# Drawing the first half of the next batch's linear attention into the last feed-forward of the batch before, with all four batches on one time axis

## The reference

```python
x = layernorm(x + linear_attention(x))       # 8 heads of 16: silu(q), silu(k), rotation, decay mask
x = layernorm(x + local_transformer(x))      # 2 layers: window attention (8 heads of 64, window 64) + gated FFN
x = layernorm(x + deformable_attention(x))   # 33 samples per token, positions computed from x, linear interpolation
x = layernorm(x + moe(x))                    # 8 experts, softmax over the sequence, top 2

# deformable attention, per batch:
pos = clip(t + (s - 16) * freq_avg[t] + phase_avg[t], 0, L - 1)      # s = 0..32
lo = floor(pos); frac = pos - lo
g = x[lo] + frac * (x[lo + 1] - x[lo])                               # a gather of rows of x
out = silu(sum_s(g * w[t, s, head]) @ out_w.T)
```

## Time and profile before

| | us |
|---|---|
| median of 3 runs | 2317.84 (2312.19 to 2323.54) |
| the profiled execution, its own time | 2323.0 |
| its span, first to last instruction | 2321.0 |
| PE / DVE / ACT / POOL busy | 1669.0 / 1307.1 / 969.2 / 1140.6 |
| of POOL's, the 1056 gathers (L744) | 1074.9 |
| mean granted TensorE clock | 0.853 |

### The profile page before, as it was taken

The page is one execution under the profiler, slowest core; times in us unless marked ns, Lnnn a source line. Parts: engine busy times, 40 slices in busy tenths (PEclk is TensorE's granted clock), DMA queues, the critical chain, the costliest instruction groups (busy, mean ns, idle before and its releaser), DMA issues.

```text
span 2321.0 us, 34040 instructions
## 1 busy us (share of the span) xinstructions
PE 1669.0 (72%) x11753; PEld 1075.6 (46%) x11753; DVE 1307.1 (56%) x2182; ACT 969.2 (42%) x2341; POOL 1140.6 (49%) x1136
## 2 busy tenths in 40 slices
PE   5667675766687767756878758667777567999967
PEld 3343333434454534435545424355445335766747
DVE  6664643567766734667577436576666344343333
ACT  3355553323445553225444623145455333343431
POOL 0000003467766516477676062776763265777710
PEclk8899997878898978779899978788998778999975
DMA  3000003223333323133333231333333252333311
GB/s 126 10 19 14 14 15 64 64 82 110 114 90 90 94 42 89 50 101 112 98 103 101 42 76 43 101 110 101 101 94 73 46 152 67 103 102 102 102 23 37
DMA packets 92404, 178.45 MB, mean 77 GB/s; under 512 B 21434, under 2 KB 49220, under 8 KB 91972
## 3 DMA queue, kind: packets, MB, share of 16 engines
q0 software_dynamic: 50688, 138.48, 21.4%
q1 hardware_dynamic: 41540, 37.70, 5.8%
HBM read 150.93 MB, written 8.92 MB: 69 GB/s over the span
## 4 chain that ended last, share of the span: by engine, by line
PE 33%; DVE 22%; POOL 15%; issue 14%; ACT 11%; DMA 4%; DVEq 0%; POOLq 0%; SPq 0%; ACTq 0%
POOL pool_c L744 14%; PE c L1591 4%; DVE pool_c L1240 4%; DMA pool_c<-rows_of_x,idx 4%; ACT prob L881 3%; DVE ssq L1144 3%; DVE nmax L1154 2%; PE pb L1491 2%; PE pa L1491 2%; DVE pool_a L1197 2%; PE tb L1372 2%; PE pb L1539 2%; PE pa L1539 2%; PE sc L1656 2%; PE pa L1529 1%
## 5 line engine op out<-in xcount | busy, mean ns | idle before, releaser
L744 POOL DMA_INDIRECT pool_c<-rows_of_x,idx x1056 | 1074.9, 1018 | 1070.7 <-issue 655.9
L1240 DVE TENSOR_TENSOR pool_c<-pool_c 128x768 f32<-128x768 f32 x352 | 341.0, 974 | 307.3 <-DMA pool_c<-rows_of_x,idx 268.5
L1591 PE MATMUL c<-ident,pool_c 128*128 128x128 f32 x2112 | 338.1, 305 | 171.3 <-DVE pool_c L1240 171.1
L1591 PEld LDWEIGHTS c<-ident,pool_c 128*128 128x128 f32 x2112 | 278.8, 158 | 298.9 <-DVE pool_c L1240 211.2
L881 ACT ACTIVATE prob<-sc,nmax 128x128 f32<-128x128 f32 x512 | 180.3, 379 | 126.9 <-DVE nmax L1154 126.8
L796 ACT COPY pool_a<-tb 128x512 f32<-128x512 f32 x188 | 112.1, 596 | 69.6 <-PE tb L1372 69.6
L1491 PE MATMUL pa<-wqkv,pool_a 128*128 128x512 f32 x192 | 115.7, 688 | 16.1 <-DVE pool_a L1197 6.9
L1491 PE MATMUL pb<-wqkv,pool_a 128*128 128x512 f32 x192 | 116.4, 693 | 13.3 <-DVE pool_a L1010 6.4
L1521 PE MATMUL ta<-vmix,pool_a 128*64 128x64 f32 x1024 | 79.0, 236 | 62.0 <-ACT pool_a L796 60.1
L881 ACT ACTIVATION_READ_ACCUMULATOR prob<-sc,nmax 128x1 f32 x512 | 111.4, 218 | 0.0
L1144 DVE TENSOR_REDUCE ssq<-pool_a 128x16 f32<-128x1024 f32 x64 | 77.7, 1214 | 57.8 <-ACT pool_a L857 57.7
(11 more groups left out here) (404 smaller groups left out, 3354.9 us busy)
## 6 DMA issues: line engine op xcount, KB each, us to landing
pool_c<-rows_of_x,idx POOLq DMA_INDIRECT x1056
vmix<-vring SPq DMA_DIRECT2D x128, 128.0 KB
rows_of_x<-x2tok SPq DMA_DIRECT2D x16, 256.0 KB
xtok<-in_x SPq DMA_DIRECT2D x4, 512.0 KB, 4.4
x_of_all<-x2tok SPq DMA_DIRECT2D x8, 256.0 KB, 2.4
out<-pool_c SPq DMA_DIRECT2D x8, 256.0 KB, 2.6
wqkv<-in_wqkv SPq DMA_DIRECT2D x1, 1536.0 KB
xtok<-x_of_all SPq DMA_DIRECT2D x3, 512.0 KB, 6.3
```

The source lines that it names most:

```text
L744: pool.indirect_dma_start(gat[:, n % GB, s, :], None, table, bass.IndirectOffsetOnAxis(ap=idx[:, t, SC * c + s:SC * c + s + 1], axis=0),). ...
L1240: V.tensor_tensor(g4, g4, wv, ALU.mult).then_inc(SEM["c_prod"], 1)
L1591: ins = mm(out[:, c:c + P], x, ident[:], start=(i == 0 and k == 0), stop=(i == BCH - 1 and k == len(parts) - 1), is_transpose=True, skip_g ...
```

## The change

All batches are put on one axis, with batch b at 29.0 x b, and the whole program is written out: the loop, its register arithmetic and its branches are gone, and every wait compares with a constant. On this axis the opening's early half stands at 20.0 to 23.0 of the batch before and its late half at 23.0 to 27.0 (that is -6.0 to -2.0 of its own batch). The head of block 1 moves to 20.8 to 22.8 and chunks 9 to 87 to 22.8 to 44.0 (-6.2 to 15.0 of the next batch). A few offsets within a tile change. x turned over gets a tensor of its own (`xin`) in place of `xb`; `pool_a` is laid out anew, so that `silu4`, `keyA`, `qryA` and `vp` lie where window attention's buffers come free first, with waits for those. The norms of the opening get semaphores of their own. Four small tensors of the mixture of experts move into `pool_a`.

```diff
-OPENING = 7.66
+PERIOD = 29.0
+OPENING, LATE_OPENING, TAIL_AT = 7.0, 4.0, 22.0
...
-    "pe": {... "O": 1.49, "turn": -0.5, ...},
-    "act": {... "rn": -1.84, "P": 1.17, ... "turn": -0.35, ...},
-    "dve": {... "rn": -1.99, ... "O": 1.45, ...},
+    "pe": {... "O": 1.46, "turn": -0.45, ...},
+    "act": {... "P": 1.17, "rn": -1.72, ... "turn": -0.3, ...},
+    "dve": {... "rn": -1.87, ... "O": 1.3, ...},
...
-HEAD_AT, GATHER_AT, GATHER_END = -6.87, -4.81, 15.0
+HEAD_AT, GATHER_AT, GATHER_END = 20.8, 22.8, 44.0
 NEXT_AT, NEXT_GATHER, NEXT_END = 17.3, 18.98, 20.78
...
+    k = opening.index(("KV",))
     for i, step in enumerate(opening):
-        out.append((-2.0 - OPENING * (1 - i / len(opening)) + at["opening"], step))
+        if i < k:
+            time = -2.0 - OPENING + (OPENING - LATE_OPENING) * i / k
+        else:
+            time = -2.0 - LATE_OPENING * (1 - (i - k) / (len(opening) - k))
+        out.append((time + at["opening"], step))
...
+    for b in range(B):
+        out += [(PERIOD * b + time, ("first", b, *step)) for time, step in first_times(e)]
+        out += [(PERIOD * b + time, ("second", b, *step)) for time, step in second_times() if b < B - 1 or time < TAIL_AT]
+    return [step for _, step in sorted(out, key=lambda x: x[0])] + tail_steps()
...
-            for s in FIRST[order]:
-                first_or_ahead(0, *s)
-            with eng.Fori(1, B) as b:
-                for part_, *s in both_steps(order):
...
+            for part_, b, *s in schedule(order):
+                if part_ == "first":
+                    first(b, *s)
...
+        silu4 = part("a", 4, BLK)
+        ktok = silu4.rearrange("p a (b c) -> p (a b) c", b=2)
         keyA = part("a", G, N)
         qryA = part("a", G, N)
-        silu4 = part("a", 4, BLK)
-        ktok = silu4.rearrange("p a (b c) -> p (a b) c", b=2)
+        vp = part("a", T, H, 2 * HD)
...
-        hT = part("b", N)
         sq = part("b", 2, BLK)
         qn = part("b", 2, HB, DH)
         r2 = part("b", 2, HB, DH)
+        hT = part("b", N)
...
-                    wait_filled(pool, ("up", LAYERS - 1, J - 1, FB - 1), b - 1)
+                    wait_filled(pool, ("O", LAYERS - 1, T - 1), b - 1)
                     nc.gpsimd.memset(vp[:], 0.0).then_inc(SEM["a_zero"], 1)
...
-                        copy_out(("xT", j), xb[:, 1 + BLK * j:1 + BLK * (j + 1)], b)
+                        if j == 0:
+                            wait_drained(act, ("ao", J - 1), b - 1)
+                        copy_out(("xT", j), xin[:, BLK * j:BLK * (j + 1)], b)
...
+                    wait(act, "b_qk", b - 1, LAYERS * T)
                     wait(act, "a_rot", b, i - 3)
...
+                    if i == 0:
+                        wait_filled(dve, ("vp", LAYERS - 1, T - 1), b - 1)
+                    elif i == 4:
+                        wait_filled(dve, ("S", LAYERS - 1, T - 1), b - 1)
                     wait_drained(dve, ("kq", i), b)
...
                 elif what == "KV":
+                    wait_filled(dve, ("up", LAYERS - 1, J - 1, FB - 1), b - 1)
```

More of the change, by code:

```diff
@@ L512, in build @@
         }
-        AHEAD = {n for n in PER if n[:2] == "c_" and not n.startswith("c_gather")}
         SEM = {n: ctx.enter_context(nc.semaphore(n)) for n in PER}
@@ L1134, in first @@
                     if l == 0:
[L1135 removed]
+                        wait_norm(dve, "out", j, b)
                     else:
```

289 lines of the change are left out of this document (128 added, 161 removed), and 6 rows, old and new, of the table AT.

## The result

The changed kernel takes 2288.19 us (median of 4 runs, 2275.92 to 2293.16), the kernel before beside it 2319.44 (2312.19 to 2323.54). The ratio is 0.9855, its 95% interval 0.9818 to 0.9891. The gain is 31 us, where 75 were predicted. The profiled execution took 2293.16 us with a span of 2291.3.

What follows compares the result with a forecast made beforehand. POOL was taken to pace `KV` to the sixth maximum except for one 37.5 us hole. Per seam -24 - 1 = -25 us, three seams -75, from 2323.0 to 2248, less 5.2 for the median: 2243 us; range 2198 to 2303.

Steps and rivals of the forecast that it cites:

- inner one: Range of the likeliest case alone, 2208 to 2285 us; that case had 58%.
- main term: Late opening: `acc` 9 moves right behind `E` 0; `KV` to sixth maximum 173 us against 197.3, 24 less per seam.
- the branches: Loop branches at the seams, removed by writing out: 1 us less per seam on average.
- hole: POOL's one gap of 37.5 us behind `KV`, waiting for PE, which reaches `acc` 9 only behind `heads` 3.
- small waits in the measured proportion: POOL's waits from `KV` to sixth maximum, scaled from 5.1 us per 38.3 chunks: 5.3 us.
- no gap over 10 us: Sign of being right: POOL has no such gap between the first row numbers and the sixth maximum.
- Early half and head: Row numbers to `KV`: four early steps save at most 5 us, block 1's head costs 6; zero, -6 to +10.
- Offsets and the last stretch: `rn` behind the copies of `P`, and the stretch after the sixth maximum: zero each.
- The rival of the slower side: `rn`'s new place lengthens every tile by up to 1.5 us, 96 us over 64 tiles: 2339 us; 9%.
- Batch 0 and tail: They hold nothing of the seam but one head: zero, -3 to +3 us.
- The opening's own chain: Rival: PE, ACT and DVE bind the opening, `KV` to projection 70 us; 2294 us with the head's full cost; 17%.
- Gathers slower beside DVE: Rival: mean gather in the denser opening rises to 1.25 us, costing 25 us more, main term gone: 2315 us; 8%.

Runs made afterwards that it cites:

- small products: The changed kernel with DVE's product of each chunk cut to its first sixth (128 values of 768 a partition): 2206.71 us, one execution.

## Why the prediction was partly right

The forecast was 75 us less, the measurement is 31 us less. The 2288 us lie inside the range of 2198 to 2303 and above the inner one of 2208 to 2285. That inner range doesn't come out of its own terms: 20 to 33 us for the main term, 1 for the branches and +2 as the middle of -6 and +10 give 2222 to 2261. Over the three seams of the profiled executions `KV` to the sixth maximum gave 36.5 us where 72 were forecast, and row numbers to `KV` took 9.6 more where 3 less were forecast. The rest of the passes gave 9.8 where zero was forecast, and batch 0 and the tail took 7.1 more. That the last two nearly cancel is luck. I had taken batch 2 for all three; batch 1's hole was 33.4 us, and it gave only 9.2.

**Direction and the bound: right.** POOL paces `KV` to the sixth maximum, except for its holes. Its rate of 4.08 us a chunk came out at 4.09, a third fewer gathers shortened the stretch by 30 us, and where the holes are closed its own work fills 175.2 of 179.2 us.

**The main term: mechanism right, size wrong.** Forecast were 173 us, made of 162.8 own work, 5.3 small waits and 5 to the restart. The trace has 183.9: 166.3, 10.8 and 6.8 (917.80 to 924.58). So -24 became -13. Of the 10.9 missing, 7.3 are waits. The step that failed is "small waits in the measured proportion". I had looked only at where `acc` 9 goes. `acc` 10 is tied to `E` 1, and so to DVE's scan: the gap of 7.02 us at 935.04. A buffer comes free where the chain of the opening lets it. The other 3.5 are 0.8 chunks more than my 39.9. The hole is not worth its length either: with both chunks put ahead, POOL waits 8.0 us less than with the head alone behind, and the stretch is 5.0 shorter in batch 2 and 2.9 in the mean, as POOL does more chunks in it. So waits and chunks aren't two separate terms, as my sum has them. My sign "no gap over 10 us" was met at 9.50 and told nothing; the length of the stretch was the test.

**Early half and head: zero forecast, +2.3 measured (+4.5 and +2.8 in batches 1 and 3).** The parts were near: I set the head at 6 us and the run has 7.3, the four early steps at 5 saved, and the kernel with the head behind is 5.2 under the 63.0 of before. The error is in what the term was held against. The head's way back into the late half costs nothing in the faster groups, so with it the order of the seam is worth 33 to 38 us, and the change gave some 20 of them away. I wrote that its removal there isn't counted, and did not ask whether it should have moved at all. The tables came to three loads more in the whole (109 for 106), and taking one away gave 0.5 us: inside the bounds. The kernel with the head behind `KV` even has 115 of them and is 16 us shorter. The Trainium skill (ScalarE: Activation LUTs, What ACT_TABLE_LOAD costs) has 2.66 us for a switch. Here all 109 loads take 1.28 us; 66 of the next instructions start within 0.03 us of the load's end, and the others wait for PE or DVE.

**Branches: right, a little small.** -3 forecast, -7 measured for the whole form (-11 to -3), in which the branches aren't told from the new layout.

**Offsets and the last stretch: zero forecast, wrong twice.** `rn` behind `P` gives about 14 us in the whole and costs 4 to 7 in batch 0. The rival of the slower side had the right place and the wrong mechanism and, for the whole, the wrong sign. `rn` isn't held up tile by tile: in 15 of batch 0's 16 tiles it starts within 0.13 us of DVE's sum. The other, at 0.8, is one in which a feed-forward has changed the table. ACT in order of time there, the changed kernel:

```profile
250.61 0.60 ACT L763 COPY pool_a<-tb 128x512 f32<-128x512 f32 x1
251.23 1.28 ACT L834 ACT_TABLE_LOAD   x1
252.53 0.22 ACT L834 ACTIVATE ssq<-ssq 128x16 f32<-128x16 f32 x1
252.76 1.28 ACT L836 ACT_TABLE_LOAD   x1
254.06 0.31 ACT L836 ACTIVATE ssq<-ssq,cols 128x16 f32<-128x16 f32 x1
```

and the kernel before:

```profile
249.50 1.28 ACT L863 ACT_TABLE_LOAD   x1
250.98 0.21 ACT L863 ACTIVATE ssq<-ssq 128x16 f32<-128x16 f32 x1 [0.20 <-DVE ssq L1146]
251.21 1.28 ACT L865 ACT_TABLE_LOAD   x1
```

Before, the first load passes while ACT waits for DVE's sum (0.20 us are left of the wait). Now the two copies stand in that wait, and the load comes behind it. That explains 0.8 us in a pass. The rest of batch 0's loss goes with a longer busy PE at a lower granted clock (0.85 for 0.97 from the first to the sixth maximum); which causes which isn't settled. Nor is it shown why the passes with gathers gain: there, too, `rn` starts right behind the sum.

**Batch 0 and tail: zero, -3 to +3.** Batch 0 +3.5 by `rn`. The tail's +3.6 isn't an effect: it is 486.3 us when the changed kernel is run again.

**The other rivals.** The opening's own chain (17%) didn't take over: the stretch from `KV` to the projection is 58.2 us and not 70. Gathers slower beside DVE (8%): the mean didn't move, so as a cause of the miss the rival is out. But the effect was in the 1043 ns from the start, as the last section shows; small products take 55 ns of it away. The Trainium skill (SBUF — State Buffer, SBUF: two separate sides) gives 3100 ns for one beside a copy. Here one gather of the changed kernel took 3.07 us, beside products and not a copy, and five of its 1056 took over 2 us; no mean over a stretch came to more than 1.1 us.

## What to carry to other kernels

A hole in the bounding engine closes only as far as the slowest list that feeds its buffers; follow every release in the hole, not the first. Closing it gives less than its length, because the engine then does more of its own work in the same stretch. When work moves between two stretches, price it in both: the same head cost 7.3 us where a chain was bound and, in the faster groups, nothing where POOL was. A step that needs another activation table can hide the load in its wait if it stands ahead of the fillers (0.8 us here), but that is one term of several: with gathers beside it, `rn` behind the fillers was the better place by some 14 us.

## What the runs showed of the hardware

The same program differs between groups of runs when gathers run. The kernel before takes 2534 and 2531 us in two of them and 2319 to 2326 in the others, while batch 0 takes 373 to 385 in all. The chip's number isn't the reason: the group with 2319 us beside the changed kernel and the last one with 2531 have the same. The kernel with the old `rn` alone ran in a group of either kind. In batch 2's pass (522.5 and 475.0 us) PE is busy 365.3 us for 335.0, at a granted clock of 0.82 for 0.88; which causes which isn't settled. POOL's waits in the kernel with the head behind `KV`, in a slower group:

```profile
POOL pool_c L711 <- issue: 272.8, 900, 1.1
POOL pool_c L711 <- PE c L1567: 264.7, 97, 11.3
POOL pool_c L711 <- remote: 80.0, 53, 3.3
```

and in a faster one:

```profile
POOL pool_c L711 <- issue: 291.1, 969, 0.3
POOL pool_c L711 <- PE c L1567: 156.7, 78, 11.0
```

In the slower group 53 gathers stand still for 1.5 us in the mean between two of the same kind, for nothing that the profile shows, and PE and DVE have such pauses too. The cause was not found.

What a gather on POOL takes goes with where the DVE instructions beside it read. In the changed kernel 260 of the 1056 gathers have no DVE instruction beside them: 945 ns in the mean, 949 at most. The 82 that have only TENSOR_TENSORs beside them with an input in PSUM take 946 ns in the mean, 983 at most. The 296 that have only TENSOR_TENSORs with both inputs in SBUF take 1112 ns in the mean, and up to 1958. The longest gather stands beside a chunk's product and rotations that follow one another without a pause (POOL's line, then DVE's of the same time):

```profile
1546.34 3.07 POOL L711 DMA_INDIRECT pool_c<-rows_of_x,idx  x1 [0.30 <-issue]
...
1546.44 0.95 DVE L1216 TENSOR_TENSOR pool_c<-pool_c 128x768 f32<-128x768 f32 x1
1547.31 1.28 DVE L1182 TENSOR_TENSOR pool_a<-pool_a,rot 128x512 f32<-128x512 f32 x2
1548.62 1.23 DVE L1185 TENSOR_TENSOR pool_a<-pool_a,rot 128x1024 f32<-128x1024 f32 x1
```

Over the 122 gathers from `KV` to the sixth maximum, 1042 for 945 ns is 12 us a seam of the engine that paces it. With the small products the mean is 987. The small products gave back some 7 of them; an arrangement that keeps the results wasn't tried.

And a logarithm and an exponential that follow each other without an explicit load take two table loads, 2.85 us apart at 892.71 and 895.56; one load of the common set ahead of them replaces both.
